# Counted semaphores instead of cleared ones, ScalarE's query squares, and a mixture of experts whose second weighting VectorE adds straight into the rows

## The reference, cut to what matters

```python
x = x + tanh(g_xattn[0]) * decayed_memory(layernorm(x), ctx, ctx)      # a running sum over time
x = x + tanh(g_ffn[0])   * L0_ffn(layernorm(x), ...)                   # 16 small experts, 2 chosen, 1 shared
x = x + tanh(g_xattn[1]) * L1_xattn(layernorm(x), ctx, ...)            # attention to the context
x = x + tanh(g_ffn[1])   * L1_ffn(layernorm(x), ...)                   # 8 experts, below
x = x + tanh(g_xattn[2]) * L2_xattn(layernorm(x), ctx, ctx, mask, ...)
x = x + tanh(g_ffn[2])   * L2_ffn(layernorm(x), ...)
x = x + tanh(g_xattn[3]) * L3_xattn(ctx, layernorm(x), mask, ...)      # perceiver: 16 heads of 64
x = x + tanh(g_ffn[3])   * L3_ffn(layernorm(x), ...)                   # attention, 8 experts, rmsnorm
```

```python
h = einsum('td,edf->etf', xt, W1) + b1[:, None, :]
h = layernorm(relu(h), g1, be1)                      # over 512
y = einsum('etf,efd->etd', h, W2) + b2[:, None, :]
y = layernorm(relu(y), g2, be2)                      # over 128
out = einsum('te,etd->td', gate, y)                  # gate: two of eight, the rest 0
```

## Time and profile before

| | us |
|---|---|
| median of 3 runs (lowest, highest) | 1697.77 (1696.64, 1699.97) |
| the profiled execution, its own time | 1694.08 |
| its span, first to last instruction | 1692.3 |
| PE, DVE, ACT, POOL busy | 1421.5, 1087.9, 736.3, 410.0 |
| a block, from one `ffn1` to the next (L994, by the trace) | 408.1, 408.5, 407.3 |

### The profile page before, as it was taken

The page is one execution under the profiler, slowest core; times in us unless marked ns, Lnnn a source line. Parts: engine busy times, 40 slices in busy tenths (PEclk is TensorE's granted clock), DMA queues, the critical chain, the costliest instruction groups (busy, mean ns, idle before and its releaser), DMA issues. The chain is left out here.

```text
span 1692.3 us, 28855 instructions
## 1 busy us (share of the span) xinstructions
PE 1421.5 (84%) x11038; PEld 930.3 (55%) x11038; DVE 1087.9 (64%) x3306; ACT 736.3 (44%) x1397; POOL 410.0 (24%) x318
## 2 busy tenths in 40 slices
PE   5788988897877988798878898879887799888977
PEld 4455744564654664366555564446555467445645
DVE  3456765777636676686754676667664667657776
ACT  0254434663334533565424543456432444345632
POOL 1121310630031230261013031055012223116300
PEclk8799999998989999999989999999898999999989
DMA  9000000000000000000000000000000000000000
GB/s 337 0 1 1 1 1 1 1 2 16 1 7 1 1 1 1 1 2 17 1 7 1 1 1 1 1 1 2 16 1 8 1 1 1 1 0 2 2 16 7
DMA packets 16824, 19.60 MB, mean 12 GB/s; under 512 B 3352, under 2 KB 15400, under 8 KB 16172
## 3 DMA queue, kind: packets, MB, share of 16 engines
q1 hardware_dynamic: 16688, 17.75, 3.1%
HBM read 16.70 MB, written 1.05 MB: 10 GB/s over the span
## 5 line engine op out<-in xcount | busy, mean ns | idle before, releaser
L251 POOL TENSOR_TENSOR root<-variance,minus_half 128x2 f32<-128x2 f32 (+1 forms) x75 | 58.2, 776 | 734.1 <-DVE variance L268 460.7
L1068 ACT ACTIVATE work<-bank,w_f 128x512 f32<-128x512 f32 x128 | 88.0, 687 | 118.4 <-PE bank L1005 118.1
L1016 PEld LDWEIGHTS bank<-w_f1d,work 128*128 128x128 f32 x1024 | 119.4, 192 | 15.3 <-issue 15.3
L1571 ACT ACTIVATE work<-work,small 128x128 f32<-128x128 f32 x256 | 78.3, 388 | 96.5 <-DVE small L1703 96.5
L1005 PE MATMUL bank<-xnT,w_f 128*128 128x512 f32 x256 | 119.8, 615 | 0.0
L1016 PE MATMUL bank<-w_f1d,work 128*128 128x129 f32 x1024 | 119.5, 275 | 0.0
L1626 POOL TENSOR_TENSOR small<-small 128x16 f32<-128x16 f32 x32 | 92.9, 2904 | 84.7 <-DVE small L1662 83.1
L1661 DVE TENSOR_REDUCE small<-work 128x16 f32<-128x1024 f32 x48 | 58.5, 1218 | 54.3 <-ACT work L1540 42.9
L1402 PE MATMUL bank<-w_x,cxT 128*128 128x512 f32 x128 | 66.5, 643 | 32.0 <-DVE work L1675 27.1
L1097 POOL TENSOR_TENSOR small<-small,minus_half 128x4 f32<-128x4 f32 x32 | 57.6, 1799 | 139.5 <-DVE small L1136 139.5
L620 DVE TENSOR_REDUCE small<-bank 128x8 f32<-128x512 f32 x96 | 65.6, 683 | 34.6 <-PE bank L487 34.6
(11 more groups left out here) (289 smaller groups left out, 3319.2 us busy)
## 6 DMA issues: line engine op xcount, KB each, us to landing
w_f<-in_f_dram SPq DMA_DIRECT2D x1, 2616.0 KB
w_f<-in_f_dram SPq DMA_DIRECT2D x1, 2180.0 KB, 26.6
w_x<-in_x_dram SPq DMA_DIRECT2D x1, 2115.0 KB
w_l<-in_l_dram SPq DMA_DIRECT2D x1, 2088.5 KB, 21.3
w_f1d<-in_f1d_dram SPq DMA_DIRECT2D x4, 512.0 KB
work<-in_x_dram SPq DMA_DIRECT2D x5, 256.0 KB, 2.8
work<-in_ctx_dram SPq DMA_DIRECT2D x5, 256.0 KB, 3.3
out_dram<-x SPq DMA_DIRECT2D x4, 256.0 KB, 2.3
```

The source lines that it names most:

```text
L1016: pe.matmul(z_of(e, t)[:, 0:129], hT[e % 2][:, c, t * P:(t + 1) * P], w_f1d[:, c, e, :], start=(c == 0), stop=(c == 3))
L1068: act.activation(hT[e % 2][:, c, :], banks[n % 3][:, :], ACT.Relu, bias=k_f1["b1"][:, n:n + 1]).then_inc(hT_ready, 1)
L1571: ins = act.activation(s_sb[b % 2][:, c * P:(c + 1) * P], s_sb[b % 2][:, c * P:(c + 1) * P], ACT.Exp, bias=negmax[b % 2][:, c:c + 1])
```

## The change

- **Semaphores are counted through.** Every semaphore has a total for a block (`rows_ready:16` and the like), and each wait is `due(sem, n)`, n plus block times total, or `ahead(sem, n)` for the next block's opening. `clear` and the blocks' own `nc.Block()` are gone: one program holds all four blocks. The totals are constants.
- **Start of a block.** `ffn0`'s transposes wait for `opened`, which `open_rows` sets; then TensorE waits for the context's copies, the values, and for `ffn3`'s additions of the block before. The copy to `x` (L909) goes: `ffn0`'s additions read `x_next` and write `x`, after the store.
- **`rms_last` of blocks 0 to 2** moves behind the first four `gate_up` of the next `ffn0`, one part behind each; POOL gives its root behind the weighting of step 1. In the last block it stays.
- **The last block** does not open a next one (`more`), and loads nothing.
- **`ffn1`**: `add` on PE goes. `times_gain(e)` multiplies by g2 at once; the weighting by `w2` (now kept for each expert, with the gate `tg` in it) follows in the next expert, behind `first_moments`, and goes into `x`. Both halves of the squares' sum come behind it, before the first root is awaited. Bank 3 holds only the biases and means and is added once, before the last expert.
- **The perceiver**: `square_queries` moves from POOL to ScalarE, behind `square_keys(1)` for tile 1, at the end of steps 0 and 2 for tiles 2 and 3.

```diff
-                    def square_queries(t):
-                        pool.wait_ge(q_copied, 2 * t + 2)
-                        pool.wait_ge(q_summed, t)
-                        pool.tensor_tensor(q_sq, q_rows[t % 2], q_rows[t % 2], ALU.mult).then_inc(q_squared, 2)
...
+                    def square_queries(t):
+                        act.wait_ge(q_copied, due(q_copied, 2 * t + 2))
+                        act.wait_ge(q_summed, due(q_summed, t))
+                        act.activation(q_sq, q_rows[t % 2], ACT.Square).then_inc(q_squared, 2)
...
-                        if e >= 1:
-                            add(e - 1)
...
+                    keep_clock(pe, banks[1], 2)
+                    pe.wait_ge(coef_ready, due(coef_ready, 1))
...
+                    for t in range(TILES):
+                        m = pe.matmul(banks[3][:, t * D:(t + 1) * D], combT[:, t * P:(t + 1) * P], w_f1b[:, :],
+                                      start=True, stop=True)
+                    m.then_inc(means_done, 1)
...
+                        if h == 5:
+                            act.wait_ge(combT_done, due(combT_done, 1))
+                            act.copy(combT, banks[0][0:16, :]).then_inc(combT_ready, 1)
...
+                    link(dve.tensor_scalar(comb, comb, tg[:, 5:6], None, ALU.mult))
...
+                    def times_gain(e):
+                        rows, gain = y[e % 2], k_f1["g2"][:, e * D:(e + 1) * D]
+                        if e < EXPERTS - 1:
+                            link(dve.tensor_tensor(rows, rows, gain.unsqueeze(1).to_broadcast([P, TILES, D]), ALU.mult))
+                        else:
+                            link.last_of([dve.scalar_tensor_tensor(rows[:, t, :], rows[:, t, :], mv[:, t, e, 0:1], gain,
+                                                                   ALU.subtract, ALU.mult) for t in range(TILES)])
+                    def second_weights(e):
+                        dve.wait_ge(second_root, due(second_root, e + 1))
+                        link(dve.tensor_tensor(w2[:, :, e], r2, comb[:, :, e], ALU.mult))
+                    def add_tile(e, t):
+                        return dve.scalar_tensor_tensor(x[:, t, :], y[e % 2][:, t, :], w2[:, t, e:e + 1], x[:, t, :],
+                                                        ALU.mult, ALU.add)
...
                     for e in range(EXPERTS):
                         first_moments(e)
+                        if e >= 1:
+                            second_weights(e - 1)
+                        if e == LAST:
+                            dve.scalar_tensor_tensor(coef[:, :, 0:LAST], mv[:, :, 0:LAST, 0], -1.0, w2[:, :, 0:LAST],
+                                                     ALU.mult, ALU.mult).then_inc(coef_ready, 1)
+                        if e >= 1:
+                            add_expert(e - 1)
+                        if e < LAST:
+                            add_squares(e + 1)
                         first_scale(e)
                         second_moments(e)
+                        times_gain(e)
+                    dve.wait_ge(means_done, due(means_done, 1))
+                    dve.wait_ge(x_added, due(x_added, LAST))
+                    dve.tensor_tensor(x[:, :, :], banks[3][:, :].rearrange("p (t d) -> p t d", t=TILES), x[:, :, :],
+                                      ALU.add).then_inc(means_added, 1)
+                    second_weights(LAST)
...
-                    dve.sem_inc(rows_ready, 2)
-                    dve.wait_ge(stored, 16 * i + 16)
-                    link(dve.tensor_copy(x[:, :, :], x_next[:, :, :]))
+                    turn_pairs(pe, None, turn_no, xn_next)
+                    pe.wait_ge(c_taken, due(c_taken, 2))
+                    pe.wait_ge(kv1.v_ready, due(kv1.v_ready, TILES))
+                    if prev is not None:
+                        pe.wait_ge(prev, 8 * i)
...
+                        if (t, g) == (0, 1) and i > 0:
+                            give_root(pool, 4)
...
+                    last_rows = iter(()) if i == 0 else rms_last(dve, link)
                         if s < n:
                             gate_up(s)
+                            some(last_rows, 1)
                             some(next_rows, 3)
+                        if s == 6 and i > 0:
+                            dve.wait_ge(stored, 16 * i)
...
-            clear(flow + opening + kv1.sems + kv2.sems + kv3.sems + [s for _, sems in stages for s in sems])
```

690 lines of the change are left out of this document (327 added, 363 removed).

## The result

The changed kernel takes **1603.29 us** (median of four runs, 1598.2 to 1605.42), where the kernel before took 1697.2 beside it (four runs, 1692.7 to 1699.97): a ratio of 0.9445, 95% interval 0.9414 to 0.9475. The forecast was 1619, with a range of 1602 to 1643. In the profiled executions the span fell from 1692.3 to 1596.4 us, by 95.9, where the sum had 78.8.

A forecast was written before the change was run, and what follows sets the result against it. No engine bounds the whole; waits in four places do: expert loop, tail of `ffn1`, perceiver's step 0, between blocks. Terms 40.0 + 13.6 + 20.1 + 0.4 + 4.7 = 78.8 off 1694.1 give 1615.3 profiled, 1619 median; range 1602 to 1643.

The forecast's parts named there:

- The loop: Expert loop of `ffn1`: the period falls from 9.04 us to TensorE's 8.00, with VectorE needing 7.65.
- The tail: End of `ffn1`, by VectorE: 7.15 us, with TensorE's means coming in time.
- `ffn1` in all: Whole expert stage, loop and tail: 10.0 us less for each block, 40.0 in all; bounds 7 and 11.5 a block.
- The perceiver: Query squares moved to ScalarE end VectorE's wait in step 0: 3.4 us for each block, 13.6 in all.
- Between blocks: From `ffn3` into the next `ffn0`: 6.7 us less at each of three ends, 20.1 in all.
- The start: From preparation to block 0: one meeting of the engines is lost, 0.4 us less; bounds 0 and 1.
- The last block: `ffn3` of the last block, which opens nothing: 4.7 us less, with TensorE the bound.
- The counters: Semaphore waits in the whole kernel: a wait for a bigger constant costs nothing; bounds -1 and 1 us.
- A: Rival in `ffn1`: POOL's roots are shut out by VectorE's additions, 5.2 us a block, 1640 us; chance 0.10.
- B: Rival between blocks: they overlap less than said, 4 to 6 us come back at three ends, about 1634; chance 0.10.
- C: Rival in the `ffn1` loop: TensorE falls to the low clock without `add`, slower, 1731 if half the time; chance 0.03.
- D: Rival for the whole change: one overlap is undone by a misread order, little over half comes, 1655; chance 0.06.

The follow-up runs named there:

- e6: The changed kernel with one more VectorE instruction, a copy of 128x128, at the end of each expert in `ffn1`: 1606.23 us, ratio 0.9443.
- e7: The changed kernel with one more TensorE filler matmul for each expert but the last, behind the sums of squares: 1636.03 us, ratio 0.9638.
- e2: The changed kernel with the old expert stage (additions by TensorE, second weighting before the next expert), in counted semaphores: 1657.29 us, ratio 0.9749.
- e9: The changed kernel, but the last block opens a next one too, which is never used: 1604.57 us, ratio 0.945.
- e4: As e3, and TensorE also waits at the start of a block until the rows of the block before are stored: 1624.93 us, ratio 0.957.
- e1: The changed kernel with the perceiver's query squares back on POOL, in the old order: 1618.5 us, ratio 0.9536.
- e3: The changed kernel with `rms_last` at the end of each block's own `ffn3` again, not in the next block's ring: 1613.84 us, ratio 0.9499.
- e8: The changed kernel with two filler matmuls ahead of the very first transposes, which moves all later work: 1603.17 us, ratio 0.9455.
- e12: The changed kernel with filler matmuls in the pauses of each attention and of each block's `ffn0`: 1611.42 us, ratio 0.9479.

## Why the prediction was right, and where its sizes were off

The forecast's steps hold, and the time fell 15.7 us below it. It is inside the range by 1.3 us, and that is luck: it lies outside the 1606 to 1632 that I gave 0.66, in the branch "more than forecast", which had 0.05. Blocks are 380.8, 381.8 and 382.0 us long from one `ffn1` to the next, not some 388. Term by term, in profiled time:

- **The loop, 8.00 us by TensorE, 7.65 by VectorE.** Right in kind: TensorE is late next, and e6 and e7 show it from both sides. Measured 7.90 and 7.59. The first period is 8.00 again, as in the earlier trace rows (9.70 in block 3, where the clock falls behind the pause in front of it); the row that I took holds a L1051 of 1.05 behind a pause, where the later ones take 0.95. So 8.00 was the period of the first expert and not of the others.
- **The tail, 7.15** (its parts add up to 7.17)**.** 7.34 to the last expert's additions (205.51 to 212.85). The means come in time, as predicted.
- **`ffn1` in all, 40.0.** 40.3, in e2 42.3. Between blocks with the same clock, 0.98, it is 90.66 before and 81.08 after, 9.6 each, so 38.3 of the 40.3 are the loop itself and 2 are clock.
- **The perceiver, 13.6.** 18.1 in this trace, and 8.5 to 16.6 in the eleven others with the same code, so that as a whole the term is about right. Its two halves were both off. The first maxima of steps 0 and 1 are 9.36 us apart, not some 11, and that in every one of these traces; before it was 13.57. That is 4.2 each and 16.8 in all, my upper bound, where I had taken 2.4 for the wait and 1.0 for the low clock behind it: the pause is down to 1.79 us, and the clock stays up there. Against that, the other traces have low stretches elsewhere, in e9 one of 3.4 us that begins 95 us into each of its first three stages, and I had no term for those. The changed kernel's has none at all, and a low stretch at the end of the third block's stage before makes the other 1.4.
- **Between blocks, 20.1.** 18.5 (`ffn3` and the next `ffn0`: 272.8 before, 254.3 after). The copy of the router's row comes 1.35 us behind the last addition, where 1.3 was said, and the ring's pause is 3.94 where 3.9 was said. Given back in the ring are 2.7 a time, not 2.2; a low stretch follows that pause, but what it costs was not measured by itself.
- **The start, 0.4.** 1.6, of which 1.3 lie ahead of the first transposes. No experiment is about it, and that stretch takes 59.9 to 62.6 us in the other traces of kernels that leave it alone.
- **The last block, 4.7.** 4.6 in the trace, in e9 as in the table.
- **The counters, nothing.** e2 agrees: the old expert stage with counted waits has full periods of 9.00 to 9.05 us where the clock is up, as before, and takes 371.5 us against 369.4. The clearing and meeting that went with the old semaphores, 2.3 us an end, had no term of their own; they lie inside the "between blocks".
- **What had no term: 12.7.** Attentions 1, 3 and 6 are 5.0, 7.4 and 2.0 shorter, `ffn2` 1.7 longer. I had carried over the clock of all stages that the change doesn't touch. They have 48 us at the low clock where they had 89. In the eight other traces with the period of 7.90 and no filler in these stages, the four take 471.8 to 484.8 us in sum, where they took 491.0 before, so some gain is in all of them, 6 to 19. This is the step that failed: the forecast priced each stage by itself, and held more than that, "down to 1595, from less low clock everywhere", at a chance of 0.05.

Of the rivals, **A** fell: L1117 starts at 167.23, just ahead of the additions at 167.26, and takes 1.01; the root is there at 168.24, and VectorE comes for it at 170.18. (L1117 starts ahead of the additions in all 28 experts that have them, so whether back-to-back additions could shut it out was hardly put to the test; L1119, which starts amid L1181's four, takes 1.04.) **B** fell too; e4 shows what it would have cost, since there TensorE does wait for the store. **C** fell: the loop's clock is 0.97, though TensorE has no `add` between. **D** fell with all four parts at their places.

The clock's part is settled only by half. That the same pauses behind the same work bring a low stretch at one time and not at another is shown, by block 0 against block 1 of attention 1 and by e9 against the changed kernel. That it is their place in time which decides is an explanation that no run here separates from others. That attention 3's gain goes with the faster loop is shown as well: in the eleven kernels with the period of 7.90 (the changed one, e1, e3 to e6, e8 to e12) it takes 30.1 us in 37 of 44 stages, and in the three with a longer one (before, e2, e7) in none of 12, where it takes 31.5 to 33.4. Why is open. A slower loop may put the stages behind it at another place on the clock's beat, or it may leave TensorE with another history; the runs can't tell these apart. Nor can single traces be leaned on here: e6, whose loop is the same as the changed kernel's, was profiled at a clock of 0.952 and 1610.6 us, and ran in 1593.2 and 1601.9 us at 0.964. The changed kernel's own profiled run, 1598.2 us at 0.964, is the quickest of its four; the others had 0.955 to 0.961. The profiled run is 5 us below the median there and 3 below it before (1694.08 against 1697.2), so some 2 us of the 95.9 in the traces are not in the medians; and which stages of the changed kernel are short is this one run's, attentions 1 and 6 perhaps among them.

## What to carry to other kernels

When an engine waits twice per turn of a loop for a short result, look for work of its own that it can put into that wait, even work that another engine did for it: moved from TensorE to VectorE, 1.1 us of additions per expert made a period of 9.04 into one of 7.90, until the other engine set it. Price what you remove between stages by the order that it forces first (5.4 us of a pause of 7.75 here), and then by its own instructions and meetings (2.3 us); and when you put a wait in its place to test this, see to it that the wait isn't as long as what it replaces. And give the clock of the untouched stages a term with bounds of its own: here it was worth 13 of 96 us in one trace, and 6 to 19 over all, and filling the pauses to win more of it won nothing that the time shows. Before you explain a stage that came out shorter, look at it in several executions of the same code.

## What the runs showed of the hardware

- Two pauses of 1.40 us each, in the same order behind the same work, had the clock fall to 1.2 GHz in one block and not in the next. Two executions of the same instructions had the first perceiver stage at 96.8 and at 98.4 us (the changed kernel, and e9, which is the same up to the last block). Over the changed kernel and the twelve made from it, the time at the low clock in the profiled runs goes from 101 to 196 us.
- POOL's root of 128x4 takes 1.01 us while VectorE is idle (the last root of `ffn3` in the kernel before). L1117, which starts just ahead of VectorE's four short additions, takes 1.01 to 1.03, and they take 1.14 as without it. Asked for while VectorE works on two inputs from SBUF, the root ends 0.86 to 0.90 us behind the instruction that runs at its start, in both traces: its time is 1.04 beside the first short one of L1171, 1.38 beside L1179, 1.91 beside L1121. The Trainium skill, "SBUF — State Buffer", section "SBUF: two separate sides", has a lock on the shared ports that is held for one instruction; L1119 ends 0.86 us behind the end of L1179, so the trace agrees.
- Clearing the semaphores at the end of block 0 was two instructions of 0.23 and 0.75 us, and with a meeting of the engines before and behind it 2.33 us from VectorE's last work to TensorE's next (2.38 and 2.31 at the other two ends). The store of 256 KB takes as long to land, 2.30 us in e4.
